# A vision tower with 16 experts: ten token tiles of up to 128 rows for eleven of 114, and expert rows as the stationary operand

## The reference, cut to what matters

```python
h = tok(x)                                   # layernorm, 768 -> 256, layernorm, + position
h = concat(cls_tok, h)                       # (32, 38, 256)
h = h + attn0(layernorm(h))                  # causal, 16 heads, quantised weights
h = h + tanh(layernorm(h) @ W @ A1 @ A2 + b)
h = h + attn1(layernorm(h))                  # 16 heads, biases
# experts: every token goes to the best of 16, at most 76 tokens per expert
score = softmax(ln(h) @ Wg + bg); idx = argmax(score); gate = max(score)
y = relu(buf @ W1[e] + b1[e]) @ W2[e] + b2[e]     # 256 -> 1024 -> 256
h = h + y[idx, pos] * gate                   # tokens beyond 76 get nothing
```

## Time and profile before

| | us |
|---|---|
| median of 3 executions | 375.3 |
| lowest and highest | 370.9, 375.43 |
| the profiled execution, its own time | 375.37 |
| its span in the trace | 373.5 |
| mean granted TensorE clock, as a share of full speed | 0.965 |

### The profile page before, as it was taken

One profiled execution on the slowest core, in us unless ns is written; L12 is line 12 of the kernel. 1 busy time (PEld: TensorE's weight loads), 2 busy tenths in 40 slices (PEclk: granted clock), 3 DMA queues, 4 the chain that ended last, 5 costly groups with the idle time before them and its releaser, 6 DMA issues.

```text
span 373.5 us, 9318 instructions
## 1 busy us (share of the span) xinstructions
PE 343.2 (92%) x3440; PEld 283.7 (76%) x3440; DVE 201.9 (54%) x576; ACT 164.6 (44%) x452; POOL 174.7 (47%) x298
## 2 busy tenths in 40 slices
PE   2969999999999999999978997767999999999983
PEld 2758888787887887878867876657988787886871
DVE  0487648675957567576686888880133213232221
ACT  1657983555575666576752647250222121210210
POOL 0257857675858476777655685651001210111112
PEclk9998999999999999999996999878899999999998
DMA  7999411101466433136312121525996599795700
GB/s 239 411 420 472 191 50 50 52 29 46 151 196 211 149 125 134 52 83 220 111 50 81 50 85 51 129 68 162 372 401 221 187 351 409 264 369 218 226 11 10
DMA packets 40348, 66.40 MB, mean 178 GB/s; under 512 B 5475, under 2 KB 31398, under 8 KB 39472
## 3 DMA queue, kind: packets, MB, share of 16 engines
q1 hardware_dynamic: 35344, 56.15, 43.4%
q10 hardware_dynamic: 2448, 7.42, 5.2%
q0 software_dynamic: 2512, 2.25, 2.3%
HBM read 54.44 MB, written 8.48 MB: 168 GB/s over the span
## 4 chain that ended last, share of the span: by engine, by line
PE 79%; DVE 7%; DMA 4%; issue 4%; SPq 2%; POOL 1%; ACT 1%; ACTq 0%; DVEq 0%; POOLq 0%
PE bank L973 16%; PE bank L986 12%; PE bank L865 9%; PE bank L841 7%; PE bank L912 6%; PE bank L926 5%; PE bank L875 4%; PE bank L893 4%; PE bank L901 3%; PE bank L933 3%; PE bank L850 2%; SPq L656 2%; PE bank L918 2%; PE bank L801 1%; DMA mid<-in_tokw 1%
## 5 line engine op out<-in xcount | busy, mean ns | idle before, releaser
L973 PEld LDWEIGHTS bank<-mid,early 128*128 128x128 f32 x512 | 59.6, 196 | 3.5 <-issue 2.8
L973 PE MATMUL bank<-mid,early 128*128 128x96 f32 x512 | 61.1, 281 | 0.6 <-ACT mid L1121 0.6
L771 POOL DMA_INDIRECT out<-mid,idx x12 | 11.8, 981 | 103.9 <-DVE mid L1290 103.9
L1130 ACT ACTIVATE mid<-bank,cols 128x96 f32<-128x96 f32 x64 | 16.6, 342 | 74.2 <-PE bank L973 74.2
L730 POOL TENSOR_TENSOR mid<-mid,tab 128x608 f32<-128x608 f32 x32 | 38.4, 1200 | 18.5 <-PE bank L893 18.3
L986 PE MATMUL bank<-early,mid 128*64 128x256 f32 (+1 forms) x448 | 43.7, 381 | 1.2 <-DVE mid L1307 1.2
L1307 DVE TENSOR_SCALAR mid<-bank,cols 128x96 f32<-128x96 f32 x64 | 15.9, 310 | 45.2 <-PE bank L973 35.4
L865 PE MATMUL bank<-xnT,attn 128*128 128x228 f32 (+1 forms) x192 | 38.5, 357 | 0.0
L986 PEld LDWEIGHTS bank<-early,mid 128*64 128x64 f32 (+1 forms) x448 | 25.7, 123 | 16.1 <-issue 3.0
L865 PEld LDWEIGHTS bank<-xnT,attn 128*128 128x128 f32 x192 | 35.3, 202 | 1.2 <-DVE tokens L1239 0.2
L841 PE MATMUL bank<-early 128*114 128x256 f32 (+1 forms) x132 | 32.1, 396 | 3.1 <-DVE tokens L1206 3.1
(11 more groups left out here) (124 smaller groups left out, 611.6 us busy)
## 6 DMA issues: line engine op xcount, KB each, us to landing
early<-in_w SPq DMA_DIRECT2D x60, 512.0 KB, 6.8
v3a<-vt SPq DMA_DIRECT2D x102, 40.0 KB
early<-vt SPq DMA_DIRECT2D x90, 40.0 KB
expert_in<-k_empty SPq DMA_DIRECT2D x1, 3084.0 KB, 37.9
attn<-in_w SPq DMA_DIRECT2D x4, 512.0 KB, 9.3
mid<-expert_in SPq DMA_DIRECT2D x6, 257.0 KB, 6.1
mid<-expert_in ACTq DMA_DIRECT2D x6, 257.0 KB, 6.5
early<-in_xt ACTq DMA_DIRECT2D x1, 1536.0 KB, 28.7
```

Of the source, the lines that this page charges most:

```text
L973: ins = mm(Hp[b][:, c // 4, (c % 4) * ECOLS:(c % 4 + 1) * ECOLS], w1s[e % SLOTS][:, kc, c * 128:c * 128 + 128], xeT[:, e, kc, :], start=kc ...
```

## The change

The change has three parts.

**Tiles.** Ten tiles (`SIZES`: eight of 128 rows, then 116 and 76) take the place of eleven. A tile now begins anywhere within an image. The value step `v` alone keeps the eleven cuts at three images (`VTILES`, `vrows`, `vcols`). The position table `added` starts at an image boundary, so for tiles 1 to 8 SP makes shifted copies of it on the chip, 16 DMAs of 64 rows each, into `attn1`, whose own load moves to a step `a1` of SP's planned list. The gain is the same in all rows; POOL instead multiplies `rs` by a mask `patch`. The count step `cnt` gets a third small matmul, since the constant rows no longer fit into the 128-row table.

**Groups.** Queries and keys come in five groups, four of 256 columns and one of 192.

**Experts.** `first_half(m)` now runs by passes, eight over a pair of experts and four over the late rows of four. The packed rows, 128 x 64 or 128 x 32, are stationary and W1 is the moving operand with 512 columns; the hidden values come out with tokens on partitions. ACT and DVE copy them to SBUF (`stage`), TensorE transposes them in eight blocks (`turn_hidden`), and ACT and DVE add the bias and apply relu (`hidden`). `second_half` has the same matmuls as before. W1 gets six slots, and there are 29 matmuls on a constant.

```diff
-TROWS = TILE_IMGS * SEQ
-TILES = -(-NIMG // TILE_IMGS)
-GROUP_IMGS = 6
-GCOLS = GROUP_IMGS * SEQ
+TROWS = 128
+SIZES = [128] * 8 + [116, 76]
+GCOLS = 2 * TROWS
-PAIR, TILE, LAYER, EAGER = 7.64, 12.23, 121.4, 401.34
+PAIR, TILE, LAYER, EAGER = 7.68, 12.18, 113.2, 632.69
...
             sp.dma_start(maskb[:, :], k["k_mask"]).then_inc(l_mask, 16)
+            sp.wait_ge(tables_ready, 1)
+            for t in range(1, TILES - 1):
+                for half in range(2):
+                    at = (PHASES[t] + 64 * half) % SEQ
+                    sp.dma_start(tables[t][64 * half:64 * half + 64, :], added[at:at + 64, :]).then_inc(phased[t > 3], 16)
             by_feature(3)
             sp.dma_start(temp_[:, 0:3 * KC * DIM], i["in_ffn0"]).then_inc(l_ffn0, 16)
             by_feature(4)
-            sp.dma_start(attn1[:, :], i["in_attn1"]).then_inc(l_attn1, 16)
...
+            for g in range(EXP // 4 - 1):
+                coming = range(4 * g + 6, min(4 * g + 10, EXP))
+                sp.wait_ge(hid_full[1], 3 * g + 3)
+                for e in coming:
+                    first(e)
+                sp.wait_ge(y_full, 3 * g + 3)
+                for e in coming:
+                    second(e)
...
+                for half in range(2):
+                    if m >= 2:
+                        pe.wait_ge(hid_staged[half], m - 1)
                     for kc in range(KC):
+                        for a, e in enumerate(experts):
+                            ins = mm(Hp[m % 2][a * width:(a + 1) * width, half, :], xeT[:, e, kc, at:at + width], w1s[e % W1_SLOTS][:, kc, half * 512:(half + 1) * 512],
+                                     start=kc == 0, stop=kc == KC - 1)
+                    ins.then_inc(hid_full[half], 1)
+            def turn_hidden(m):
+                for half in range(2):
+                    pe.wait_ge(hid_staged[half], m + 1)
+                    if m:
+                        pe.wait_ge(hid_ready[half], m)
+                    for c in range(HC // 2):
+                        ins = tr(Tp[half][:, c * 128:(c + 1) * 128], staged[m % 2][:, (half * HC // 2 + c) * 128:(half * HC // 2 + c + 1) * 128], ident)
+                    ins.then_inc(hid_turned[half], 1)
...
-            for n in range(24):
+            for n in range(29):
...
+            for g in range(EXP // 4):
+                if g:
+                    first_half(3 * g)
+                first_half(3 * g + 1)
+                turn_hidden(3 * g)
+                ...
+                first_half(3 * g + 2)
+                turn_hidden(3 * g + 1)
+                second_half(3 * g)
+                turn_hidden(3 * g + 2)
+                second_half(3 * g + 1)
+                second_half(3 * g + 2)
...
+            def hidden(m):
+                experts, width, at = members(m)
+                act.wait_ge(hid_turned[0], m + 1)
                 for c in range(HC // 2):
+                    for a, e in enumerate(experts):
+                        ins = eng.activation(hT[:, m % 2, c, a * width:(a + 1) * width], Tp[0][:, c * 128 + a * width:c * 128 + (a + 1) * width], ACT.Relu,
+                                             bias=b1T[:, e * HC + c:e * HC + c + 1])
+                ins.then_inc(hid_ready[0], 1)
...
+            def hidden(m):
+                link(eng.tensor_tensor(to, Tp[1].rearrange("p (c e n) -> p c e n", c=HC // 2, e=n), bc(bias, 3, width), ALU.add))
+                eng.tensor_scalar(hT[:, m % 2, HC // 2:, :], hT[:, m % 2, HC // 2:, :], 0.0, None, ALU.max).then_inc(hid_ready[1], 1)
```

More of the change, by code:

```diff
@@ L37 @@
 TILE_IMGS = 3
-TROWS = TILE_IMGS * SEQ
-TILES = -(-NIMG // TILE_IMGS)
-GROUP_IMGS = 6
-GCOLS = GROUP_IMGS * SEQ
-GROUPS = -(-NIMG // GROUP_IMGS)
+VTILES = -(-NIMG // TILE_IMGS)
+TROWS = 128
+SIZES = [128] * 8 + [116, 76]
+TILES = len(SIZES)
+STARTS = [sum(SIZES[:t]) for t in range(TILES)]
+PHASES = [start % SEQ for start in STARTS]
+GCOLS = 2 * TROWS
+GROUPS = -(-NTOK // GCOLS)
 PAIRS = NIMG // 2
@@ L221, in last_pair, with pairs_of, tiles_of, group_of_pair @@
 def last_pair(t):
-    return min((TILE_IMGS * t + TILE_IMGS - 1) // 2, PAIRS - 1)
+    return (STARTS[t] + rows(t) - 1) // PCOLS
+def pairs_of(t):
+    return range(STARTS[t] // PCOLS, last_pair(t) + 1)
+def tiles_of(u):
+    return [t for t in range(TILES) if STARTS[t] < u * TILE_IMGS * SEQ + vrows(u) and STARTS[t] + rows(t) > u * TILE_IMGS * SEQ]
+def group_of_pair(p):
+    return ((p + 1) * PCOLS - 1) // GCOLS
 def needs():
@@ L570, in v_spread_count @@
         def v_spread_count(u):
-            return sum(16 * 3 * (rows(v % TILES) // SEQ) for v in range(u % 2, u + 1, 2))
+            return sum(16 * 3 * (vrows(v % VTILES) // SEQ) for v in range(u % 2, u + 1, 2))
         def v3(image, count):
@@ new lines, in _ @@
+            act.wait_ge(pair_turned, 1)
+            take_pair(Yp[0], 0, 1)
+            stage(0)
+            act.wait_ge(pair_turned, 2)
+            take_pair(Yp[1], 1, 1)
+            for g in range(EXP // 4):
+                if g:
+                    stage(3 * g)
+                stage(3 * g + 1)
+                hidden(3 * g)
+                if g < EXP // 4 - 1:
+                    act.wait_ge(pair_turned, g + 3)
+                    take_pair(Yp[(3 * g + 1) % 2], 2 * g + 2, 2)
+                stage(3 * g + 2)
+                hidden(3 * g + 1)
+                hidden(3 * g + 2)
@@ L1321, in _, with result @@
-            pair(EXP // 2 - 1)
-            lates(EXP // 4 - 1)
+            def result(m):
+                t = xe_tile(m)
+                dve.wait_ge(y_full, m + 1)
+                eng.scalar_tensor_tensor(out=xe[:, t, 0:DIM], in0=Yp[m % 2][:, 0:DIM], scalar=xe[:, t, 2 * DIM + 1:ROW], in1=xe[:, t, 0:DIM],
+                                         op0=ALU.mult, op1=ALU.add).then_inc(y_summed, 1)
+            stage(0)
+            take_late(Yp[0], 0)
+            for g in range(EXP // 4):
+                if g:
+                    stage(3 * g)
+                stage(3 * g + 1)
+                hidden(3 * g)
+                if g < EXP // 4 - 1:
+                    take_late(Yp[3 * g % 2], g + 1)
+                stage(3 * g + 2)
+                hidden(3 * g + 1)
+                for part in range(3):
+                    residual(3 * g + part)
+                result(3 * g)
+                hidden(3 * g + 2)
+                result(3 * g + 1)
+                result(3 * g + 2)
```

377 lines of the change are left out of this document (190 added, 187 removed), and 6 rows, old and new, of the table GOAL.

## The result

| | us |
|---|---|
| before, median of 4 runs beside the changed kernel | 374.89 |
| after, median of 4 runs (359.68 to 363.00) | **361.49** |
| ratio, with its 95% interval | 0.967 (0.960 to 0.974) |
| the profiled execution of after, its own time and span | 363.0 and 361.2 |

The change saves 13.4 us where 12.5 were forecast. In the experiments one execution each of kernels 2 and 3, and one of the kernel before in two of the batches, ran 1.5 to 2% longer at a lower granted clock, and all medians and ratios there leave them out.

What follows compares the result with a forecast made beforehand. TensorE was taken to bound the kernel, fully from 40 to 180 us and from 260 us, partly between. Experts -6.2, tiles -7.8 and transfers +1.5 sum to -12.5 us: 375.4 becomes 363 us, range 354 to 371.

Steps and rivals of the forecast that it cites:

- The first half, -16.9 us: Experts on TensorE: 12 passes of 3.47 us, 41.7 us, replace 16 first halves of 3.66 us, 58.6 us.
- The rival without side by side: Experts' first half: 512 columns do not run side by side, total above 400 us; chance 0.02.
- Transposes and changes, +10.6 and +1.1: Experts on TensorE: 96 added transposes at 0.11 us, and 12 more changes between kinds of work.
- Hidden values, 0: Experts: copies, bias and relu on ACT and DVE are hidden behind other matmuls; no cost, 2 us for the range.
- That rival (390 us): Experts: hidden values come late, TensorE waits in every pass and the clock falls, about 390 us; chance 0.06.
- The start of the experts, -1.0: Experts' start: more constant matmuls close a gap, -1.7 us; one more wait for a copy, +0.6; ends +1 and -2.
- the sum: Whole kernel: experts -6.2, tiles -7.8, transfers +1.5, together -12.5 us, giving 363 us.
- predicted -6.2: The expert part as a whole: matmuls, transposes, changes and start together save 6.2 us.
- The early transfers, +1.5: Kernel start: SP's 16 copies delay tiles 4 to 6 and the feed-forward weights, stalling TensorE about 2 us, partly recovered.
- the upper end of +6: Early transfers: range 0 to +6 us, the top being the stall and a slow stretch of matmuls after it.
- Tiles and groups, -7.8: TensorE before the experts: one tile less and fewer query and key groups save 7.8 us; ends -4.5 and -10.
- better than the sum: Rival: the middle stage tightens with every engine's load and the clock stays up at the experts, about 357 us; chance 0.17.

Runs made afterwards that it cites:

- kernels 2 and 3: 2: changed kernel with the old expert part, 368.86 us; 3: changed kernel with feed-forward weights and tiles 4 to 6 ahead of the table copies, 356.38 us.
- kernel 6: The kernel before with only the changed kernel's planner numbers (PAIR, TILE, LAYER, EAGER, GOAL, COST): 370.96 us beside 374.46, ratio 0.992.
- kernels 10 and 11: Changed kernel, first half of each pass: 10, each expert gives all eight instructions before the next, 392.48 us; 11, six each, then two each, 377.55 us.
- kernel 8: The changed kernel with every transpose of hidden values done twice, 96 more: 371.07 us, ratio 0.989.
- Kernel 5: The changed kernel with SP's copies in two lots: six for tiles 1 to 3, feed-forward weights, tiles 4 to 6, other ten copies, tiles 7 to 9: 355.03 us.

## Why the prediction was right, and where it was not

The totals of this section are sums from each start to the next start over the whole expert part of one execution.

**The first half, -16.9 us: right in kind, 1.1 us too large.** A place of 512 columns costs 0.43 us as taken, shared by two or four. The sixteen old first halves take 60.0 us, and 58.3 where the clock stays up (kernel 6; 58.6 were taken). The twelve passes take 42.5 us, 3.54 each, where 3.47 was taken. The rival without side by side is out; kernels 10 and 11 show what would have brought part of it on, the order of the list.

**Transposes and changes, +10.6 and +1.1: right.** The twelve blocks of eight take 12.0 us with their changes, and 96 more cost 10.5 us (kernel 8). The changes around the packed rows' transposes add another 0.4 us.

**Hidden values, 0: right.** ACT's 128 small operations (`L1209` of after) are busy for 25.8 us, 0.20 each where 0.26 was taken, and covered; no pass but the first two waits. That rival (390 us) is out.

**The start of the experts, -1.0: right in kind, 0.5 us too small.** The first pass goes at full speed, 3.65 us. Before, the first first half took 5.41 us where kernel 6 takes 3.78, which is the 1.7 us between 60.0 and 58.3. Two waits for copies, 0.46 and 0.24, stand for one of 0.56. That is -1.5 us.

**One wait that the sum did not have.** In the kernel before TensorE waits once more, ahead of the last second halves, for DVE's hidden values:

```profile
360.41 7.26 PE L986 MATMUL bank<-early,mid 128*64 128x256 f32 x96 [1.18 <-DVE mid L1307]
```

In after there is no such wait, 1.2 us less.

From the first packed transposes to the end there are 107.6 us for 113.75: **-6.15, predicted -6.2**. The agreement is closer than the terms deserve. TensorE's own work fell by 3.4 us (-15.8, +12.0, +0.4) where the sum has 5.2; the faster start (1.5 for 1.0) and the wait that went away (1.2 for nothing) made up for it.

**The early transfers, +1.5: too small, by some 5 us.** This is the step that failed. The chain was named rightly (copies on SP, then `in_ffn`, TensorE at its fifth step), and its issue times were even too late (23.5 us, not 26). Two terms were undersized. "By 25 us I take everything ahead as landed" was wrong: the copies took 6.9 to 12.2 us from issue to landing, the last of them issued at 22.2 us, and the last two of ACT's patch loads, issued from 5.98 us on, took 19.7 us at the median. The weights landed 11.1 us after their issue. The sum gives 5.5 us to their own bytes and those of tiles 4 to 6, and 2, at most 4, to the delay; here some 6 us went on it, with 389 GB/s moving in this stretch (share 1.05). And the slow stretch after the wait was only an end of the range: `L881` cost 1.9 us more than its usual 1.89, `L897` 0.8. That is 4.0 + 1.9 + 0.8, some 6.7 us, beyond the upper end of +6. Kernel 5, which takes away most of the stall, is 5.9 us ahead behind these matmuls and 6.5 us faster at the end; that agrees with the size.

**Tiles and groups, -7.8: the work is gone, the total came out larger.** The matmuls on the constant begin at 243.88 us instead of 250.02, 6.1 us earlier, in spite of some 6.7 us lost at the start. So the rest was shortened by about 13: the 7.8 of the sum and 5 more. By the spread of this boundary that 5 is uncertain by 2 to 3 us. Its cause is mostly open. The planner's new numbers, which I had counted as nothing, are worth 3.5 us on the old kernel (kernel 6), but its timeline has only 1.4 us ahead of the matmuls on the constant, and the 1.6 of the faster first pass is already in the experts' term. The rest may be the lighter load of DVE and POOL, which the rival "better than the sum" gave as its cause, or the new order on the new tiles; no run has the new tiles with the old numbers.

So 363 was met within 1.5 us because -5 and +5 cancelled, which is luck. The experts' 6.2 us were built on rows of nearly the same operations, and each of their terms held within 1.2 us; the transfer term rested on a delay for which there was no row.

## What to carry to other kernels

Small copies out of SBUF on a queue that still feeds the first tiles are paid by the loads behind them: issue only those whose readers come first, then the loads, then the rest (6.5 us here). When narrow operands share the array, interleave them in the list: with up to four 512-column instructions per operand in a row nothing was lost here, with six and eight the partner started late. And price a change's new table of planner numbers by itself, on the old kernel, before crediting the work that was removed; then look in the timeline where its gain lies, so that it is not counted twice.

## What the runs showed of the hardware

- Side by side does not need neighbouring instructions. With at most four 512-column instructions per group of columns in a row, two or four groups start within 0.06 us; with six, the partner starts two places later, with eight, four places (passes of 3.6, 4.5 and 5.35 us for a pair; 3.6, 6.2 and 8.8 for four). That it is a queue of four per group is a reading that fits three kernels; a run of five was not tried.
- A copy of 64 partitions out of SBUF takes SP 0.63 us from one issue to the next. That is not dearer than a load: the loads of 128 partitions from DRAM on the same queue took 0.38 to 0.74.
- A stall at the start cost 4.0 us of waiting and 2.7 more of slow matmuls. Behind the wait the granted clock was at the lower level, 1.2 GHz (the stretch from 35 to 40 us of after, columns as above):

```profile
35.00:40.00 5.00, 5.00 (x13) 3.95 (x13) 0.00 (x0) 1.47 (x4) 0.58 (x2) 0.51 1.09 444
```

Eight matmuls of 256 columns took 3.78 us there and 1.89 in before, where TensorE had not waited just ahead of them.

- The length of a rest does not alone tell what follows: after 1.65 us the first pass was slow in before (5.41 us for 3.78 in kernel 6) and at full speed in kernel 8.
